# Two graph attention layers on one core: four edits to an already tuned kernel (looks moved, one subtraction moved to GpSimd, the maximum spread later, a new order at the end)

## The reference, cut to what matters

```python
def layer0(h, adj, a):                    # 4096 nodes, 64 features
    e = (h @ a1)[:, None] + (h @ a2)[None, :]
    e = where(e > 0, e, 0.01 * e)
    e = where(adj > 0, e, -9e15)
    return softmax(e, axis=1) @ h
def layer1(h, adj, W, a):                 # slope 0.2, elu at the end
    Wh = h @ W
    ...
    return elu(softmax(scores, axis=1) @ Wh)
x = layernorm(x + layer0(x, adj, a))
x = layernorm(x + layer1(x, adj, W, a))
```

## Time and profile before

| | us |
|---|---|
| median of 3 runs | 446.12 (444.03 to 446.91) |
| the profiled execution | 444.36 |
| its span, first to last instruction | 442.4 |
| PE busy | 408.1 (92%) |
| DVE busy | 378.9 (86%) |
| ACT busy | 384.1 (87%) |
| POOL busy | 251.8 (57%) |
| granted TensorE clock, mean | 0.991 |

### The profile page before, as it was taken

One profiled execution on the slowest core, in us unless ns is written; L12 is line 12 of the kernel. 1 busy time (PEld: TensorE's weight loads), 2 busy tenths in 40 slices (PEclk: granted clock), 3 DMA queues, 4 the chain that ended last, 5 costly groups with the idle time before them and its releaser, 6 DMA issues.

```text
span 442.4 us, 11826 instructions
## 1 busy us (share of the span) xinstructions
PE 408.1 (92%) x4484; PEld 397.1 (90%) x4484; DVE 378.9 (86%) x682; ACT 384.1 (87%) x591; POOL 251.8 (57%) x292
## 2 busy tenths in 40 slices
PE   1599899999999999999998998999999999999980
PEld 1488899999999999999998998999999999999880
DVE  4799897898989989889899988888888888898963
ACT  3898997979979798797998989999999999999820
POOL 5533263763737547295492145677776868685921
PEclk9999999999999999999999999999999999999996
DMA  5999979799897998989510000000000000000000
GB/s 116 100 107 107 91 66 98 62 103 83 74 101 62 98 86 71 88 71 88 80 52 1 1 25 2 1 25 1 27 1 25 0 24 0 24 1 25 2 25 16
DMA packets 22766, 22.48 MB, mean 51 GB/s; under 512 B 1344, under 2 KB 22464, under 8 KB 22720
## 3 DMA queue, kind: packets, MB, share of 16 engines
q0 software_dynamic: 17424, 16.78, 43.7%
q1 hardware_dynamic: 4208, 4.05, 2.8%
q10 hardware_dynamic: 1088, 1.05, 0.7%
HBM read 69.30 MB, written 2.10 MB: 161 GB/s over the span
## 4 chain that ended last, share of the span: by engine, by line
PE 69%; DVE 19%; issue 7%; POOL 1%; DMA 1%; ACT 1%; DVEq 0%; POOLq 0%
PE acc L1207 62%; PE tb L1131 5%; DVE neg L819 4%; DVE pos L830 3%; DVE mask_t L745 2%; PE srcb L1141 1%; DVE scr L845 1%; DMA mask_t<-in_x 1%; DVE split L802 1%; DVE mask_t L802 1%; DVE wmov L808 1%; ACT neg L656 1%; DVE odd L730 1%; DVE mask_t L901 1%; PE pg L1175 1%
## 5 line engine op out<-in xcount | busy, mean ns | idle before, releaser
L1207 PE MATMUL acc<-wmov,pos 128*128 128x195 bf16 x2048 | 363.8, 248 | 7.8 <-DVE pos L830 5.2
L1207 PE MATMUL acc<-wmov,neg 128*128 128x195 bf16 x2048 | 364.0, 249 | 0.0
L656 ACT ACTIVATE neg<-srcb,dcol 128x512 int8<-128x512 f32 x512 | 357.5, 933 | 4.5 <-PE acc L1207 4.3
L1207 PEld LDWEIGHTS acc<-wmov,pos 128*128 128x128 fp8e4 x2048 | 201.7, 98 | 14.4 <-DVE pos L830 9.7
L1207 PEld LDWEIGHTS acc<-wmov,neg 128*128 128x128 fp8e4 x2048 | 200.7, 98 | 2.3 <-issue 1.3
L830 DVE TENSOR_TENSOR pos<-neg,mask_t 128x1024 uint16<-128x1024 uint16 x128 | 104.9, 819 | 17.8 <-PE acc L1207 5.8
L819 DVE TENSOR_TENSOR neg<-neg,mask_t 128x1024 uint16<-128x1024 uint16 x128 | 104.6, 818 | 10.0 <-ACT neg L656 7.2
L482 POOL DMA_DIRECT2D enc<-in_adj x31 | 24.7, 799 | 62.2 <-PE tb L1131 59.0
L745 DVE TENSOR_SCALAR mask_t<-tb 128x512 uint32<-128x512 uint32 (+1 forms) x64 | 43.8, 684 | 9.8 <-PE tb L1131 9.8
L1131 PE MATMUL tb<-ident,enc 128*128 128x128 f32 x256 | 39.3, 277 | 2.1 <-DMA enc<-in_adj 2.1
L730 DVE SCALAR_TENSOR_TENSOR odd<-mask_t,odd 128x1024 uint32<-128x1024 uint32 x32 | 39.3, 1228 | 0.0
(11 more groups left out here) (133 smaller groups left out, 277.9 us busy)
## 6 DMA issues: line engine op xcount, KB each, us to landing
enc<-in_adj POOLq DMA_DIRECT2D x31, 512.0 KB, 8.5
mask_t<-in_x ACTq DMA_DIRECT2D x4, 256.0 KB, 5.7
x_rows<-xout SPq DMA_DIRECT2D x8, 128.0 KB, 3.5
resid<-x_rows SPq DMA_DIRECT2D x8, 128.0 KB, 2.1
out<-xout SPq DMA_DIRECT2D x8, 128.0 KB, 1.7
wmov<-mask_t SPq DMA_DIRECT2D x2, 390.0 KB, 3.7
enc<-in_adj POOLq DMA_DIRECT2D x2, 256.0 KB, 8.2
resid<-in_a SPq DMA_DIRECT2D x1, 64.0 KB, 4.6
```

Of the source, the lines that this page charges most:

```text
L656: ins = nc.scalar.activation(neg[:, k % SR, :, b], srcb[:, q % 2, :], ACT.Sign, bias=dcol[:, layer, c:c + 1])
L1207: ins = nc.tensor.matmul(acc[t][:, side * WC:(side + 1) * WC], m[:, t * P:(t + 1) * P, b], wmov[:, c, side * WC:(side + 1) * WC], start=fi ...
```

## The change

- **Looks.** `LATE_LOOKS` becomes (2, 4, 5, 6), for supertiles 2 to 6 of layer 1 alone: four looks each instead of three, and none in supertiles 1 and 7. There are 20 as before.
- **Group 5 (the sixth) of layer 1.** Its first subtraction moves from VectorE to GpSimd, in `change_layers`; VectorE's second one moves from the end of layer 0 to step 2 of layer 1's supertile 0, and ScalarE's copy from step 1 to step 2. `subtracted(n)` counts `w_vec` accordingly. ScalarE's copy of group 3 now stands behind its copy of turned rows.
- **Maximum spread.** `spread_stat(1)` moves from before step 1 of layer 0's supertile 6 into the middle of it, and `take_max` with its `centre` from step 1 to step 2.
- **End.** TensorE runs the last two steps for tiles 0 and 1 first, then both steps for tile 2, then for tile 3. The flags of rows without neighbours are kept from layer 0 (`lone`), GpSimd multiplies them by the mean ahead of time (`lone_mean`), and tile 3 is scaled by VectorE instead of ScalarE. `finish` waits for GpSimd's reads of `part` only.

```diff
-LATE_LOOKS = {1: (2, 4, 6), NQ - 1: (1, 2)}
+LATE_LOOKS = (2, 4, 5, 6)
...
+                both = parts_of(1, MIDDLE)
+                pool.wait_ge(poss, KB * NQ)
+                pool.wait_ge(w_prod[MIDDLE % 2], (NQ + MIDDLE) // 2 + 1)
+                nc.gpsimd.tensor_tensor(both[:, :, :, 1, :], both[:, :, :, 0, :], top_of(1, MIDDLE)[:, :, :, 0, :],
+                                        ALU.subtract).then_inc(w_mid, 1)
                 multiply(pool, nc.gpsimd, 1, 6)
...
+            pool.wait_ge(mean_set, 2)
+            pool.wait_ge(lone_set, 1)
+            pool.wait_ge(turned, KB * NQ)
+            nc.gpsimd.tensor_tensor(lone_mean, wide(lone[:, :], F), meanv[:, :].unsqueeze(1).broadcast_to([P, TI, F]),
+                                    ALU.mult).then_inc(lone_mean_set, 1)
...
-                        if k in (0, 1, 6):
-                            keep_parts(1, {0: 4, 1: 5, 6: 6}[k])
+                        if k in (0, 2, 6):
+                            keep_parts(1, {0: 4, 2: 5, 6: 6}[k])
...
                         set_scur(NQ + 1, 1, 1)
+                        weigh(1, MIDDLE)
                     if k == 3:
+
+                        nc.vector.tensor_copy(lone[:, :], zero_row).then_inc(lone_set, 1)
...
-                        steps = LATE_LOOKS[NQ - 1 if is_last(q) else 1]
-                        if k in steps:
-                            look(3 * q + (LATE - 3 + steps.index(k)))
+                        if k in LATE_LOOKS and not (is_second(q) or is_last(q)):
+                            look(4 * q - 8 + (LATE + LATE_LOOKS.index(k)))
...
-                        if k >= STAGED + 2:
+                        if STAGED + 2 <= k < MIDDLE + 2:
                             weigh(1, k - 2)
...
                             spread_max(1)
+                        if k == 2:
                             take_max(1)
                             centre(1, 0, NB * EARLY)
...
-                nc.vector.tensor_scalar(zero_row, num[:, :, F], LEAST, None, ALU.is_lt).then_inc(rows_end, 1)
+                nc.vector.tensor_tensor(den, num[:, :, F], lone[:, :], ALU.add).then_inc(rows_end, 1)
+                dve.wait_ge(lone_mean_set, 1)
+                nc.vector.tensor_tensor(numf, numf, lone_mean, ALU.add).then_inc(rows_end, 1)
                 dve.wait_ge(rows_end, 1)
-                nc.vector.tensor_tensor(den, num[:, :, F], zero_row, ALU.add).then_inc(rows_end, 1)
-                nc.vector.tensor_tensor(tmpf, wide(zero_row, F), meanv[:, :].unsqueeze(1).broadcast_to([P, TI, F]), ALU.mult)\
-                    .then_inc(rows_end, 1)
...
+            def last_two_steps():
+
+                u = KB * (2 * NQ - 1) + KB - 2
+                pe.wait_ge(poss, u + 1)
+                for t in range(TI // 2):
+                    one_tile(t, KB - 2)
+                pe.wait_ge(poss, u + 2)
+                for t in range(TI // 2):
+                    one_tile(t, KB - 1).then_inc(acc_ready, 1)
+                one_tile(2, KB - 2)
+                one_tile(2, KB - 1).then_inc(acc_ready, 1)
+                one_tile(3, KB - 2).then_inc(mm_done, 1)
+                one_tile(3, KB - 1).then_inc(mm_done, 1)
```

More of the change, by code:

```diff
@@ L714, in _ @@
             act.wait_ge(pdone[1], EPI[1] * (NQ - 1))
-            for t in range(TI):
+            for t in range(TI - 1):
                 act.wait_ge(tile_summed, t + 1)
@@ L1212, in products, with one_tile @@
                 ins.then_inc(mm_done, 1)
+            def one_tile(t, k):
+                for b in range(NB):
+                    c = NB * k + b
+                    for side, m in enumerate((pos8[:, k % MR], neg8[:, k % SR])):
+                        last = k == KB - 1 and b == NB - 1 and side == 1
+                        ins = nc.tensor.matmul(
+                            acc[t][:, side * WC:(side + 1) * WC], m[:, t * P:(t + 1) * P, b],
+                            wmov[:, c, side * WC:(side + 1) * WC], start=False, stop=last, skip_group_check=True)
+                return ins
+            def last_two_steps():
[10 more added lines that the diff above has]
+                one_tile(3, KB - 1).then_inc(mm_done, 1)
             def mean_pass(i):
@@ L1276, in body @@
                             spread_rows(NQ, 0)
-                    products(layer, q, k, between)
+                    if layer == 1 and is_last(q) and k >= KB - 2:
+                        if k == KB - 2:
+                            last_two_steps()
+                    else:
+                        products(layer, q, k, between)
             all_supertiles(pe, body)
```

64 lines of the change are left out of this document (39 added, 25 removed).

## The result

| | before | changed |
|---|---|---|
| median of 20 runs each | 444.11 us | 445.73 us |
| lowest and highest | 443.43 to 446.91 | 444.87 to 448.48 |
| the profiled execution | 444.36 us | 446.03 us |
| its span | 442.4 us | 444.4 us |

The ratio is 1.0033, with a 95% interval from 1.0018 to 1.0047. The changed kernel is about 1.5 us slower. The forecast was 1.95 us faster. The median of 20 runs of the kernel before lies 2 us under that of the three first shown, so the two medians above are the ones to compare.

A forecast was written before the change was run, and what follows sets the result against it. TensorE was taken to bound layer 1 at 22.58 us per middle supertile, the VectorE-GpSimd loop close behind at 22.4. Terms -0.45 - 0.6 - 0.3 + 0.9 - 1.0 - 0.5 = -1.95 took 446.12 to 444.2 us, range 441.5 to 446.8.

The forecast's parts named there:

- the looks in supertiles 2 to 6: Layer 1: each added look makes the VectorE-GpSimd loop 0.25 us too long; cost 0.9 us, bounds 0 and 5.65.
- The rival of the blocked look: Supertiles 2 to 6: GpSimd blocks each added look, 0.42 us more; 3.05 us lost, 446.3 us in all; chance 0.15.
- No slack usable: Steps 5 to 6 of supertiles 2 to 6: each look costs its whole 1.13 us; 448.9 us in all; chance 0.08.
- Hidden looks: Supertiles 2 to 6: idle time hides the looks, cost 0, and the front yields more; 442.3 us; chance 0.20.
- Group 5: Change to layer 1: sums end earlier and `pos` of step 4 comes 0.63 us earlier; gain 0.6, bounds 0 and 1.4.
- the rival on the front: Wait leaving steps 0 and 1 returns at 2 to 4; later `dcen` eats the spread's gain; 445.2 us; chance 0.12.
- Maximum spread: Layer 0, supertile 6: TensorE no longer waits for `gst` before step 1; gain 0.45 us, bounds 0.2 to 0.55.
- Supertile 1 and supertile 7: Layer 1, looks removed: stall at supertile 2's start goes, gain 0.3 us; stalls in supertile 7 shrink, gain 1.0.
- The stall behind `judge`: Layer 1, supertile 7: `judge` takes 1.90 us between steps 3 and 4 and leaves a stall of about 0.5.
- End: After the last matmul: the division's last product starts about 0.5 us sooner; bounds 0.3 and 0.8.

The follow-up runs named there:

- experiment 3: The changed kernel with the five looks at step 5 replaced by a reduce with one SBUF input; 442.57 us, ratio 0.9963.
- experiment 5: experiment 1 with GpSimd's subtraction for group 5 waiting one `pos` longer, so that it runs beside the sums; 441.73 us, ratio 0.9951.
- experiment 12: The kernel before with the group 5 edit alone, GpSimd's subtraction beside the sums, ScalarE's moved copy included; 443.21 us, ratio 0.9988.
- experiment 10: The kernel before with the later maximum spread alone; 443.96 us, ratio 1.0002.
- experiment 11: The kernel before with the five looks of supertiles 1 and 7 left out, not moved; 443.06 us, ratio 0.9982.
- experiment 4: The changed kernel with the look of step 5 moved to step 7; 442.58 us, ratio 0.9969.
- experiment 6: The changed kernel with the old looks and without the group 5 edit, leaving maximum spread and end; 443.94 us, ratio 1.0005.
- experiment 7: The changed kernel with looks at steps 2, 4 (supertile 1), 2, 4, 6 (2 to 6), also 7 (2, 4, 6); 441.11 us, ratio 0.9931.
- experiment 9: experiment 7 with GpSimd waiting one `pos` longer before its subtraction for group 5; 441.16 us, ratio 0.9936.
- experiment 1: The changed kernel with its looks where they were before, the other three edits kept; 442.44 us, ratio 0.9966.
- experiment 2: The kernel before with the changed kernel's looks and nothing else; 446.52 us, ratio 1.0056.
- experiment 8: The kernel before with the edits at its end alone; 444.59 us, ratio 1.0026.

## Why the prediction was wrong

**The failing step is the one on the looks in supertiles 2 to 6**, "it gets 0.29 us too long; I take 0.25, because `neg` of step 6 [...] then falls where GpSimd has finished and may shrink toward 0.69". The term was +0.9 and measured +4.2. The plain time of a look was nearly right: with this look taken off the ports the period was 22.85, 0.27 over 22.58, and the whole term 1.5 us instead of 0.9. Wrong was where GpSimd would be. I took its end at 374.9 as given, though the look itself moves that end: L390 was held off for a microsecond, GpSimd ended 379.02 - 362.25 = 16.8 us behind the start of the sums and not 374.89 - 359.14 = 15.75, and `neg` and `pos` of step 6 took 0.35 and 0.30 us more instead of less. Even by the old end the reason didn't hold: with the look at 373.1 to 374.3, as the prediction itself has it, `neg` starts near 374.2, well before 374.9. In the measured rows it starts 377.25 - 362.25 = 15.00 us behind the sums, again ahead of 15.75. Of the 3.3 us by which the term was too small, the ports are 2.7 and the look's own time 0.6 (experiment 3).

**The rival of the blocked look** had the rule and the wrong victim. It priced a look held off by GpSimd, 0.42 us; what happened is a GpSimd operation held off by the look, which then cost 0.65 us in the rows downstream and 0.57 in the period. The period for which I said "reaches 23.2 and more (blocked)" was measured at 23.47 in supertile 5. With 0.57 for its 0.42 that rival would have given 5 x 0.82 - 0.3 = 3.8 us lost, near the measured 4.2. Against it I had set that "the later `neg` and `pos` are then free of GpSimd", and the rows show the opposite.

**No slack usable** priced each look at 1.13 us; measured is 0.89 in the period, so some of the slack was used. But it is more than the 0.63 us from which that rival would make the kernel slower. **Hidden looks** would have kept the period at 22.58.

**Group 5:** -0.6 forecast, +0.05 measured. The mechanism and the size held once the subtraction stood beside the sums (experiments 5 and 12, 0.58 and 0.60 us in that stretch). The step that failed is that GpSimd's subtraction was priced on GpSimd alone ("so it is hidden"). The prediction had said that sums leave it alone because PSUM is their input, but its wait let it start two operations before the sums. What came out is one half of the rival on the front, "the wait that leaves steps 0 and 1 returns at steps 2 to 4": 0.67 us left at step 0 and 0.67 came on top at step 4. Its other half, a `dcen` that eats the gain of the spread, didn't show.

**Maximum spread:** -0.45 forecast and -0.44 measured in its place. ScalarE didn't hold step 4. What the prediction lacked is what is given back 43 us later in supertile 7 of layer 0, 0.45 us in the changed kernel and 0.30 in experiment 10, whose ratio is 1.0002.

**Supertile 1 and supertile 7:** -0.3 and -1.0 forecast, -0.4 and -1.4 measured, the second near the upper bound. The stall behind `judge`, 0.5 by the forecast, doesn't exist. It isn't there in experiment 11 either, where `judge` stays and TensorE comes to the supertile without a wait: all steps up to 5 start 2.77 us apart.

**End:** -0.5 forecast, 0.66 us measured from the last matmul to the division, inside the bounds; from the issue of the store to the end of the span it was another 0.25 less.

**The sign.** With the measured middle in the forecast's sum, -1.95 - 0.9 + 4.2 = +1.35 us, against a measured +1.5. The predicted 444.2 came from a median 2 us too high for this kernel. That the measured 445.73 lies inside the stated range is therefore luck: the reasoning itself missed by 3.6 us, from -1.95 to +1.6.

## What to carry to other kernels

When an instruction is put into an idle time of one engine, ask first which ports it shares with the engine that works there, and in both directions: who is held off by it, and what that one, now late, will meet next. A gap measured in the trace is free only for an operation that leaves the neighbour's end where it was. Here a form that reads one SBUF tensor, or a place where the neighbour is waiting, was worth 0.57 us for each supertile. And an edit's own place can show exactly what was forecast while the time doesn't move, so the places where two engines meet within a tenth of a microsecond are to be compared over the whole trace.

## What the runs showed that I had not expected

- An operation of 0.74 us on GpSimd was drawn at 1.72 when a 1.21 us look of VectorE began 0.08 us ahead of it, and was undisturbed (0.74) behind a reduce of the same length.
- A near tie between the two engines tips TensorE's time by 1.35 us: with `pos` first at 410.69 the stalls of supertile 7 sum to 1.52 us, with GpSimd first at 410.75 they sum to 2.87, in programs that agree to 0.01 us over the five supertiles before.
- A second tie lies in layer 0's supertile 7, at step 3, between `neg` and an operation of GpSimd that start within 0.01 us of each other. The kernel before and then the changed one, VectorE and GpSimd:

```profile
221.27 1.28 DVE L819 TENSOR_TENSOR neg<-neg,mask_t 128x1024 uint16<-128x1024 uint16 x1
...
221.26 0.73 POOL L358 TENSOR_TENSOR scr<-scr 128x256 f32<-128x256 f32 x1
...
221.26 0.69 DVE L847 TENSOR_TENSOR neg<-neg,mask_t 128x1024 uint16<-128x1024 uint16 x1
...
221.26 1.29 POOL L368 TENSOR_TENSOR scr<-scr 128x256 f32<-128x256 f32 x1
```

- That tie sorts all fourteen traces. Where `neg` is the undisturbed one (the changed kernel and experiments 3, 4, 6, 7, 9 and 10, all with the new spread), GpSimd's work behind it comes later, and TensorE waits 1.68 to 1.83 us at step 6. Where GpSimd is undisturbed (the kernel before and experiments 1, 2, 5, 8, 11 and 12), that wait is 0.83 us or none. Experiments 1 and 5 have the new spread too, so it doesn't decide alone; what does is below 0.01 us and stays open.
- Among the latter the wait is none in experiments 1, 5 and 12, which have ScalarE's copy of group 3 behind its copy of turned rows. GpSimd's product waits for that copy: it begins at 235.80 in experiment 1 instead of 234.73, and `pos` of step 6 takes 0.69 us instead of 1.43. A wait of 0.60 us at step 7 takes back a part. The prediction had no term for this edit, and no run has it alone.
- In the traces the two ties are what makes experiments 6 and 8 no faster than the kernel before: 1.35 us are lost in supertile 7 of layer 1 in both, ahead of 0.9 to 1.0 us won at the end with the store, and in experiment 6 another 0.30 in layer 0.
